# A feature-crossing tower: layer 0's sums as full matmuls, its last tile beside a half tile of layer 1, and another front

## The chip, the cores and the metric

The kernel runs on one core of one Trainium2 chip. The metric is the device time of one execution in microseconds, lower is better. Its engines are TensorE (PE in the profile, its weight loads PEld), VectorE (DVE), ScalarE (ACT), GpSimd (POOL) and SyncE (SP), which here only issues DMAs. SP, ACT and POOL each issue DMAs in their own order; each engine works through its instructions in program order.

## The reference, cut to what matters

512 rows, 39 fields, each looked up in a table of its own: `e` is 512 x 39 x 16.

```python
z0 = einsum('bid,bjd->bdij', x0, x0)           # 39*39 products
cur0 = relu(einsum('bdk,kl->bld', z0, W0))      # l = 128
next_h, direct0 = split(cur0, 2, axis=1)        # 64 and 64
z1 = einsum('bid,bjd->bdij', x0, next_h)        # 39*64 products
cur1 = relu(einsum('bdk,kl->bld', z1, W1))
z = sum(concatenate([direct0, cur1], axis=1), axis=-1)
h = concatenate([z, dense_ctx], axis=1)         # 192 + 16
h = relu(h @ W_top1 + b_top1); h = relu(h @ W_top2 + b_top2); y = h @ W_top3
```

## The kernel before, in words

The batch is cut into 16 chunks (`CHUNKS`) of 32 rows; with 16 components each, a chunk has N = 512 columns. In every chunk:

- **Bringing x.** GpSimd gathers 11 times per chunk into `found` (L282; 117 partitions = 3 sets of 39 fields). ScalarE's `split` (L289) rounds it to `found_hi`, VectorE's `split` (L393) makes `found_lo`, the rest. SP lays high part, low part and the full values out in a DRAM buffer `x_rows` (`lay_out` L190, six DMAs; `full_rows` L213, three), and reads from it twice: `place` (L199) brings both parts to `x_parts` in four DMAs, and `widen` (L224) copies four fields at a time to 64 partitions each in `x_wide`, six DMAs of 512 KB per chunk. Buffers are three deep. `bring` (L244) is one chunk's `lay_out`, `full_rows` and `place`.
- **Layer 0.** It rests on squares: a product of two fields is had from the square of their sum. `add_up` (L476) makes sums of pairs of fields on PE with a 0/1 matrix, two tiles ("a duo") at a time: each of the two matmuls has 64 rows only, since the fields are placed so that one half of the partitions serves each tile; the seventh tile takes all 128 rows. ScalarE's `square` (L296) squares them to SBUF and `contract0` (L489) contracts them with `w0`, both operands float32. `evict0` (L303) makes `h` (twice, on both halves) and `direct`.
- **Layer 1.** 20 tiles in five groups of four. VectorE's `multiply` (L415) makes z = x * h for a group. x comes from `x_wide` (groups 0, 2, 4) or from PSUM, where PE's `spread_out` (L499, four matmuls of 32 rows) puts it (groups 1, 3). For groups 0 to 3 ScalarE makes `z_hi` (`high_part` L320) and VectorE `z_lo` (`low_part`), and PE contracts z_hi with w1_hi and w1_lo (`contract1_hi` L510, eight matmuls) and z_lo with w1_hi (`contract1_lo` L521, four). Group 4 is taken whole in float32 (`contract1_whole` L529). z, z_hi and z_lo are rings of three. 39 x 64 rows are 19.5 tiles, so the 20th is half zeros. `evict1` and two reductions on VectorE end the chunk.
- **Order.** It is written out by hand for every engine. PE works in group g of chunk c on layer 1 of c and on layer 0 of c+1: one duo's `contract0` and the next duo's `add_up` in each of groups 0 to 3. A low part is contracted one group after its high part. ScalarE has `split(1)` ahead of `evict0(0)` in the front, and `split(c+3)` at the end of group 4 of chunk c.
- **End.** `hid1_of`, `hid2_of` and `y_of` (L537 to L569) are the three top layers, for 480 columns early (their first layer inside chunk 15) and for the last 32 late.

## Time and profile before

| | |
|---|---|
| median of 3 runs | 449.84 us (449.59 to 449.95) |
| the profiled execution | 449.96 us, of which the span is 448.1 |
| PE busy | 91% of the span |
| VectorE, ScalarE, GpSimd busy | 78%, 51%, 60% |
| moved by DMA | 64.03 MB, mean 143 GB/s |

The span is what the profiler records from the first instruction to the last. An engine's busy time says how much of it the engine worked, not whether the end waited for it; that is told by the chain of work that ended last. The timeline gives the start and the length of instructions; the length of a matmul includes its way through the array, so what it takes in a row of its like is read from the distance of the starts. The granted clock of PE is 1.00 for 2.4 GHz and 0.50 for 1.2 GHz.

### The profile page before, as it was taken

The page shows a single profiled execution, that of the slowest core. Times are in us where ns is not written, and L with a number is a line of the kernel's source. Part 1 is how long each engine was busy: PE and PEld are TensorE (multiplying, and loading weights), DVE is VectorE, ACT ScalarE, POOL GpSimd, SP SyncE. Part 2 cuts the span into 40 slices and gives each one's busy share as a digit, 9 for nine tenths or more (in the row PEclk, how much of TensorE's full clock was granted, in tenths as well). Part 3 has the DMA queues.
Part 4 walks back from the last instruction along what each step waited for, and adds up shares of the span by engine and source line. Part 5 has one row for each costly group of instructions (what it writes and reads, how often), then busy time and mean ns, then how long its engine had stood idle before and what let it go on. Part 6 is the DMA issues. An engine that isn't in the chain of part 4 may idle for free.

```text
span 448.1 us, 4257 instructions
## 1 busy us (share of the span) xinstructions
PE 405.8 (91%) x1446; PEld 238.8 (53%) x1446; DVE 347.6 (78%) x197; ACT 227.2 (51%) x224; POOL 270.8 (60%) x180
## 2 busy tenths in 40 slices
PE   0263299999999999999999999999999999999997
PEld 0221056565656565656565565656565656565744
DVE  0301676998989898989898989899898989998900
ACT  2122346556464646465564655655646464645413
POOL 5777888888888888888888888888810000000000
PEclk9958589999999999999999999999999999999999
DMA  8369269493959495868668596959493949752000
GB/s 286 97 152 182 43 145 186 108 213 84 216 117 216 100 205 107 198 136 196 133 155 171 138 193 143 188 125 208 98 211 84 218 96 212 165 129 59 1 0 0
DMA packets 25740, 64.03 MB, mean 143 GB/s; under 512 B 8512, under 2 KB 16661, under 8 KB 19446
## 3 DMA queue, kind: packets, MB, share of 16 engines
q1 hardware_dynamic: 19128, 60.55, 60.4%
q0 software_dynamic: 5632, 1.35, 3.2%
q10 hardware_dynamic: 958, 1.86, 1.2%
q8 instruction: 11, 0.18, 0.2%
q14 instruction: 11, 0.09, 0.1%
HBM read 59.87 MB, written 3.84 MB: 142 GB/s over the span
## 4 chain that ended last, share of the span: by engine, by line
PE 87%; issue 8%; SPq 4%; DMA 0%; ACT 0%
PE acc L495 22%; PE acc L525 14%; PE acc L517 13%; PE acc L518 13%; PE acc L533 12%; PE sums L485 5%; PE spread L506 3%; PE spread L562 2%; SPq L243 1%; SPq L232 1%; SPq L195 1%; SPq L221 0%; PE sums L551 0%; PE sums L553 0%; SPq L205 0%
## 5 line engine op out<-in xcount | busy, mean ns | idle before, releaser
L282 POOL DMA_INDIRECT found<-in_table_dram,rows_sb x176 | 270.6, 1538 | 56.6 <-issue 53.0
L423 DVE TENSOR_TENSOR z_lo<-z,z_hi 128x2048 fp32r<-128x2048 f32 x64 | 146.2, 2285 | 2.3 <-ACT z_hi L325 1.3
L325 ACT ACTIVATE z_hi<-z 128x2048 fp32r<-128x2048 f32 x64 | 122.3, 1911 | 16.8 <-DVE z L415 15.0
L415 DVE TENSOR_TENSOR z<-x_wide,h 128x2048 f32<-128x2048 f32 x48 | 109.8, 2288 | 12.5 <-ACT h L309 8.7
L495 PE MATMUL acc<-squares,w 128*128 128x512 f32 x224 | 114.7, 631 | 0.0
L517 PE MATMUL acc<-z_hi,w_hi 128*128 128x512 f32 x256 | 106.9, 417 | 0.7 <-ACT cur L318 0.7
L518 PE MATMUL acc<-z_hi,w_lo 128*128 128x512 f32 x256 | 100.3, 392 | 0.0
L301 ACT ACTIVATE squares<-sums 128x1024 f32<-128x1024 f32 x64 | 58.8, 919 | 78.7 <-PE sums L485 70.7
L525 PE MATMUL acc<-z_lo,w_hi 128*128 128x512 f32 x256 | 90.5, 475 | 0.0
L415 DVE TENSOR_TENSOR z<-spread,h 128x2048 f32<-128x2048 f32 x32 | 73.1, 2283 | 1.3 <-PE spread L506 1.2
L525 PEld LDWEIGHTS acc<-z_lo,w_hi 128*128 128x128 f32 x256 | 47.0, 188 | 32.3 <-issue 26.8
L495 PEld LDWEIGHTS acc<-squares,w 128*128 128x128 f32 x224 | 39.7, 194 | 37.9 <-issue 36.5
L533 PE MATMUL acc<-z,w_sb 128*128 128x512 f32 x128 | 57.5, 592 | 0.0
L517 PEld LDWEIGHTS acc<-z_hi,w_hi 128*128 128x128 f32 x256 | 48.4, 189 | 15.5 <-issue 3.9
L518 PEld LDWEIGHTS acc<-z_hi,w_lo 128*128 128x128 f32 x256 | 48.3, 189 | 13.9 <-issue 3.9
L485 PE MATMUL sums<-x_parts,select_sb 64*128 64x512 f32 (+1 forms) x112 | 31.9, 507 | 23.7 <-DMA x_parts<-x_rows 22.2
L398 DVE TENSOR_TENSOR found_lo<-found,found_hi 117x176 fp32r<-117x176 f32 x16 | 5.5, 343 | 45.4 <-issue 23.6
L485 PEld LDWEIGHTS sums<-x_parts,select_sb 64*128 64x128 f32 (+1 forms) x112 | 12.4, 191 | 47.5 <-issue 46.9
L533 PEld LDWEIGHTS acc<-z,w_sb 128*128 128x128 f32 x128 | 24.3, 190 | 24.3 <-issue 23.0
L308 ACT ACTIVATE h<-acc 64x512 f32<-64x512 f32 x16 | 9.5, 593 | 52.5 <-PE acc L495 52.5
L318 ACT ACTIVATE cur<-acc 128x512 f32<-128x512 f32 x16 | 9.6, 598 | 34.2 <-issue 20.0
L434 DVE TENSOR_REDUCE feat_a<-cur 128x32 f32<-128x512 f32 x16 | 10.9, 681 | 8.7 <-ACT cur L318 8.7
(41 smaller groups left out, 111.2 us busy)
## 6 DMA issues: line engine op xcount, KB each, us to landing
x_wide<-x_rows SPq DMA_DIRECT2D x96, 512.0 KB
x_parts<-x_rows SPq DMA_DIRECT2D x62, 64.0 KB
found<-in_table_dram,rows_sb POOLq DMA_INDIRECT x176
w_sb<-in_w_dram SPq DMA_DIRECT2D x1, 1280.0 KB, 7.2
x_rows<-found_hi SPq DMA_DIRECT2D x32, 26.8 KB
x_rows<-found SPq DMA_DIRECT2D x32, 26.8 KB
x_rows<-found_lo SPq DMA_DIRECT2D x30, 26.8 KB
z<-in_select_dram ACTq DMA_DIRECT2D x1, 576.0 KB, 7.9
```

Source lines behind the costliest of these rows:

```text
L282: pool.indirect_dma_start(out=found[:, b, s * D:s * D + D], out_offset=None, in_=table, in_offset=bass.IndirectOffsetOnAxis(ap=rows_sb[:, ...
L301: nc.scalar.activation(squares[:, q % RING0, 0:n, :], sums[:, 0:n, :], ACT.Square).then_inc(squared, 1)
L325: nc.scalar.activation(z_hi[:, n % RING], z[:, n % RING], ACT.Copy).then_inc(hi_done, 1)
L415: nc.vector.tensor_tensor(z[:, n % RING], x, h[:, c % 2, :].unsqueeze(1).to_broadcast([P, QUADS, N]), ALU.mult).then_inc(multiplied, 1)
L423: nc.vector.tensor_tensor(z_lo[:, n % RING], z[:, n % RING], z_hi[:, n % RING], ALU.subtract).then_inc(lo_done, 1)
L485: last = nc.tensor.matmul(sums[:, a, :], select_sb[rows, t, :], x_parts[rows, c % BUFS, :], start=True, stop=True)
L495: last = nc.tensor.matmul(acc0[:, :], w0[:, t, :], squares[:, q % RING0, a, :], start=(t == 0), stop=(t == T0 - 1))
L506: last = nc.tensor.matmul(spread[:, q, :], select_sb[rows, T0 + i, :], x_parts[rows, c % BUFS, :], start=True, stop=True)
L517: nc.tensor.matmul(acc1[:, :], w1_hi[:, t, :], z_hi[:, r, a, :], start=(t == 0), stop=False)
L518: last = nc.tensor.matmul(acc1[:, :], w1_lo[:, t, :], z_hi[:, r, a, :], start=False, stop=False)
L525: last = nc.tensor.matmul(acc1[:, :], w1_hi[:, QUADS * g + a, :], z_lo[:, r, a, :], start=False, stop=False)
L533: last = nc.tensor.matmul(acc1[:, :], w1_sb[:, VT + a, :], z[:, r, a, :], start=False, stop=(a == QUADS - 1))
```

## The change: what it does

- x_parts is placed otherwise (`STEP`, `rows_of`): the fields of every quarter of the partitions overlap, and each field has its two parts in at least one. `add_up` takes all 128 rows for every tile, so that the matmuls of a duo follow each other on the full array.
- The squares' tiles are filled densely (`pairs`): six full ones, and a seventh with 12 pairs, which stand in rows 64 to 127. `contract0` of the seventh tile has 64 rows, as has its `square`. It is called within `contract1_whole`, right behind the half tile of layer 1, which now takes rows 0 to 63 alone; the whole group is group 2 now, not 4.
- The groups whose x comes from PSUM are 0 and 3. The order of layer 0's steps moves by one duo: in groups 0 and 1 the duos 1 and 2 of chunk c+1 are contracted, in group 2 the last tile, in group 4 duo 0 of chunk c+2. The low part of group 4 is contracted in the next chunk, and in the last chunk between the two halves of `hid2_of`.
- `found` has three planes (high, low, full). `lay_out` writes all three with one DMA for each set (3 instead of 9), `place` takes two DMAs instead of four; both wait for the low part. `x_rows` has a 40th row, which a DMA fills once.
- The front: `keep_busy` puts 30 matmuls ahead of chunk 0's first sum and 14 behind its `contract0`; `evict0(0)` stands ahead of `split(1)`; `split(1)` on VectorE stands behind `multiply(0)`; the high part of group 0 is contracted before chunk 1's sums; the third `widen` of chunk 0 comes after `bring(1)`.

```diff
--- before.py
+++ after.py
...
+STEP = 8
...
-QSTART = [0, 16, 7, 23]
...
-SPREAD = [1, 3]
-WIDE = [0, 2, 4]
-SPREAD_FROM = [0, 24, 12, 36]
...
+SPREAD = [0, 3]
+WIDE = [1, 2, 4]
+SPREAD_FROM = [0, 4, 32, 12]
+WIDE_FROM = [[8, 16], [28, 35], [20, 24]]
...
+WHOLE = 2
...
+def rows_of(f):
+    return [2 * QUADS * (f - STEP * q) + 2 * q for q in range(QUADS) if 0 <= f - STEP * q < 2 * STEP]
...
+    order = [(f, f) for f in range(F)] + [(i, j) for i in range(F) for j in range(i + 1, F)]
+    return [order[P * t:P * t + P] for t in range(T0)]
...
-        def lay_out(queue, c, half):
-            b = c % BUFS
-            queue.wait_ge((found_hi_done, found_lo_done)[half], c + 1)
-            for s, w in enumerate(SET_COLS):
-                queue.dma_start(x_rows[b, half, :, GW * s:GW * s + w],
-                                (found_hi, found_lo)[half][F * s:F * s + F, b, 0:w].bitcast(F32)
-                                ).then_inc(rows_out[b], 16)
...
-        def place(queue, c, quads):
-            b = c % BUFS
-            queue.wait_ge(rows_out[b], 16 * 6 * uses(c))
-            for q in quads:
-                start = x_rows[b, 0, QSTART[q], 0:1]
-                queue.dma_start(x_parts[32 * q:32 * q + 32, b, :].bitcast(F32),
-                                bass.AP(start.tensor, start.offset, [[N, QF], [F * N, 2], [1, N]])
-                                ).then_inc(placed[b], 16)
...
+            def lay_out(c):
...
-                sp.wait_ge(gathered[b], 16 * SLOTS * uses(c))
-                if c >= BUFS:
-                    for i in range(len(WIDE)):
-                        sp.wait_ge(wide_in[i], 32 * (c - BUFS + 1))
+                sp.wait_ge(found_lo_done, c + 1)
                 for s, w in enumerate(SET_COLS):
-                    sp.dma_start(x_rows[b, 2, :, GW * s:GW * s + w],
-                                 found[F * s:F * s + F, b, 0:w]).then_inc(full_out[b], 16)
+                    start = x_rows[b, 0, 0, GW * s:GW * s + 1]
+                    sp.dma_start(bass.AP(start.tensor, start.offset, [[N, F], [FR * N, 3], [1, w]]),
+                                 found[F * s:F * s + F, b, :, 0:w]).then_inc(rows_out[b], 16)
+            def place(c):
+                b = c % BUFS
+                sp.wait_ge(rows_out[b], 16 * SETS * uses(c))
+                for half in range(2):
+                    start = x_rows[b, half, 0, 0:1]
+                    sp.dma_start(x_parts[half:P:2, b, :].bitcast(F32),
+                                 bass.AP(start.tensor, start.offset, [[N, 2 * STEP], [STEP * N, QUADS], [1, N]])
+                                 ).then_inc(placed[b], 16)
...
+            def bring(c):
+                if c >= BUFS:
+                    sp.wait_ge(placed[c % BUFS], 32 * uses(c - BUFS))
+                    sp.wait_ge(multiplied, G * (c - BUFS + 1))
+                lay_out(c)
+                if c >= BUFS:
+                    sp.wait_ge(spread_done, len(SPREAD) * (c - BUFS + 1))
+                    sp.wait_ge(summed, ND * (c - BUFS + 1))
+                place(c)
...
-            for i in range(len(WIDE)):
-                widen(0, i)
+            sp.wait_ge(filler_in, 16)
+            bring(0)
+            widen(0, 0)
+            widen(0, 1)
             bring(1)
+            widen(0, 2)
             bring(2)
...
-                    pool.wait_ge(full_out[b], 16 * SETS * uses(c - BUFS))
+                    pool.wait_ge(rows_out[b], 16 * SETS * uses(c - BUFS))
                 for s in range(SLOTS):
...
             def split(c):
                 b = c % BUFS
                 act.wait_ge(gathered[b], 16 * SLOTS * uses(c))
-                if c >= BUFS:
-                    act.wait_ge(rows_out[b], 16 * 6 * uses(c - BUFS))
-                nc.scalar.activation(found_hi[:, b, :], found[:, b, :], ACT.Copy).then_inc(found_hi_done, 1)
+                nc.scalar.activation(found[:, b, 0, :].bitcast(F32R), found[:, b, 2, :],
+                                     ACT.Copy).then_inc(found_hi_done, 1)
...
                 n = len(DUOS[q % ND])
+                rows = slice(0, P) if n == 2 else slice(HALF, P)
                 act.wait_ge(summed, q + 1)
                 if q >= RING0:
                     act.wait_ge(contracted0, q - RING0 + 1)
-                nc.scalar.activation(squares[:, q % RING0, 0:n, :], sums[:, 0:n, :], ACT.Square).then_inc(squared, 1)
+                nc.scalar.activation(squares[rows, q % RING0, 0:n, :], sums[rows, 0:n, :], ACT.Square).then_inc(squared, 1)
             def evict0(c):
...
             act.dma_start(base_sb[:, :], base).then_inc(ids_in, 16)
             act.dma_start(select_in, select).then_inc(select_in_done, 16)
+            filler = x_rows[0, 0, F, 0:1]
...
             split(0)
-            lay_out(act, 0, 1)
-            place(act, 0, [2, 3])
             for d in range(ND):
                 square(d)
+            evict0(0)
             split(1)
-            evict0(0)
             high_part(0)
+            high_part(1)
             square(ND)
+            square(ND + 1)
             for c in range(CHUNKS):
                 for g in range(G):
                     n = G * c + g
                     if g == 0 and c:
                         evict1(c - 1)
-                    if n == 0:
+                    if g < 2 and c + 1 < CHUNKS:
+                        square(ND * (c + 1) + 2 + g)
+                    if g > 2 and c + 2 < CHUNKS:
+                        square(ND * (c + 2) + g - 3)
+                    if 0 < n < G * CHUNKS - 1 and is_v(n + 1):
+                        high_part(n + 1)
+                    if g == 2 and c + 1 < CHUNKS:
+                        evict0(c + 1)
+                    if n == 1:
                         split(2)
-                    if c + 1 < CHUNKS and g < ND - 1:
-                        square(ND * (c + 1) + g + 1)
-                    if c + 1 < CHUNKS and g == ND - 1:
-                        evict0(c + 1)
-                        if c + 2 < CHUNKS:
-                            square(ND * (c + 2))
-                    if n + 1 < G * CHUNKS and is_v(n + 1):
-                        high_part(n + 1)
                     if g == G - 1 and c + BUFS < CHUNKS:
                         split(c + BUFS)
-                    if c == CHUNKS - 1 and g >= 2:
-                        for m in [[0], [1], [2, 3]][g - 2]:
+                    if c == CHUNKS - 1 and g > 2:
+                        for m in [[0, 1], [2, 3]][g - 3]:
                             hid1_act(m, early)
...
+            hid2_act(0, early)
             evict1(CHUNKS - 1)
-            for m in range(M2 // P):
-                hid2_act(m, early)
+            hid2_act(1, early)
...
             dve.wait_ge(mixed, 1)
-            nc.vector.tensor_copy(w0[0:32, 0, :], acc1[0:32, 0:P]).then_inc(w0_ready, 1)
-            nc.vector.tensor_copy(w0[0:F - 32, 1, :], acc1[32:F, 0:P]).then_inc(w0_ready, 1)
...
                                     ALU.subtract).then_inc(w1_lo_ready, 1)
-            split(1)
             dve.wait_ge(select_ready, 1)
             multiply(0)
-            reduce0(0)
+            split(1)
             for c in range(CHUNKS):
                 for g in range(G):
                     n = G * c + g
@@ -462,6 +446,8 @@
                     if is_v(n):
                         low_part(n)
                     if n == 0:
+                        reduce0(0)
+                    if n == 1:
                         split(2)
...
-                for a, t in enumerate(tiles):
-                    rows = slice(HALF * a, HALF * a + HALF) if len(tiles) == 2 else slice(0, P)
-                    last = nc.tensor.matmul(sums[:, a, :], select_sb[rows, t, :], x_parts[rows, c % BUFS, :],
+                for a, t in enumerate(DUOS[q % ND]):
+                    last = nc.tensor.matmul(sums[:, a, :], select_sb[:, t, :], x_parts[:, c % BUFS, :],
                                             start=True, stop=True)
                 last.then_inc(summed, 1)
+            def keep_busy(acc, count):
+                for _ in range(count):
+                    nc.tensor.matmul(acc[:, :], select_sb[:, 0, :],
+                                     select_sb[:, 0:N // P, :].rearrange("p t m -> p (t m)"), start=True, stop=True)
...
                 pe.wait_ge(squared, q + 1)
+                rows = slice(0, P) if d < ND - 1 else slice(HALF, P)
                 for a, t in enumerate(DUOS[d]):
-                    last = nc.tensor.matmul(acc0[:, :], w0[:, t, :], squares[:, q % RING0, a, :],
+                    last = nc.tensor.matmul(acc0[:, :], w0[rows, t, :], squares[rows, q % RING0, a, :],
                                             start=(t == 0), stop=(t == T0 - 1))
...
-            def contract1_whole(n):
+            def contract1_whole(n, beside):
                 r = n % RING
                 pe.wait_ge(multiplied, n + 1)
-                for a in range(QUADS):
+                nc.tensor.matmul(acc1[:, :], w1_sb[0:HALF, VT, :], z[0:HALF, r, 0, :], start=False, stop=False)
+                if beside is not None:
+                    contract0(beside)
+                for a in range(1, QUADS):
                     last = nc.tensor.matmul(acc1[:, :], w1_sb[:, VT + a, :], z[:, r, a, :],
-                                            start=False, stop=(a == QUADS - 1))
+                                            start=False, stop=False)
                 last.then_inc(contracted1, 1)
...
             last.then_inc(mixed, 1)
             pe.wait_ge(select_ready, 1)
+            keep_busy(acc0, 30)
             add_up(0)
-            pe.wait_ge(w0_ready, 3)
-            spread_out(SPREAD[0])
+            spread_out(0)
+            pe.wait_ge(w0_ready, 2)
...
+            keep_busy(acc1, 14)
...
                     n = G * c + g
-                    if (n + 2) % G in SPREAD and SPREAD[0] < n + 2 < G * CHUNKS:
+                    if n == 0:
+                        contract1_hi(0)
+                        add_up(ND)
+                        add_up(ND + 1)
+                        contract0(ND)
+                    elif g == 0:
+                        contract1_lo(n - 1)
+                    if (n + 2) % G in SPREAD and n + 2 < G * CHUNKS:
                         spread_out(n + 2)
-                    if n == 0:
-                        add_up(ND)
-                    if c + 1 < CHUNKS and g < ND:
-                        if ND * (c + 1) + g + 1 < ND * CHUNKS:
-                            add_up(ND * (c + 1) + g + 1)
-                        contract0(ND * (c + 1) + g)
+                    if g < 2 and c + 1 < CHUNKS:
+                        add_up(ND * (c + 1) + 2 + g)
+                        contract0(ND * (c + 1) + 1 + g)
+                    if g > 2 and c + 2 < CHUNKS:
+                        add_up(ND * (c + 2) + g - 3)
+                    if g == G - 1 and c + 2 < CHUNKS:
+                        contract0(ND * (c + 2))
                     if c == CHUNKS - 1 and g >= 2:
                         for m in [[0], [1], [2, 3]][g - 2]:
                             hid1_of(m, early)
-                    if n and is_v(n - 1):
+                    if g and is_v(n - 1):
                         contract1_lo(n - 1)
-                    if is_v(n):
+                    if n and is_v(n):
                         contract1_hi(n)
-                    else:
-                        contract1_whole(n)
-            for m in range(M2 // P):
-                hid2_of(m, early)
...
```

## Rows read from the trace of the kernel before

**Rows 1.** The page: span, TensorE's busy share, its granted clock in 40 slices.

```profile
span 448.1 us, 4257 instructions
...
PE 405.8 (91%) x1446; PEld 238.8 (53%) x1446; DVE 347.6 (78%) x197; ACT 227.2 (51%) x224; POOL 270.8 (60%) x180
...
PEclk9958589999999999999999999999999999999999
```

**Rows 2.** The page: the chain that ended last, shares by engine.

```profile
PE 87%; issue 8%; SPq 4%; DMA 0%; ACT 0%
```

**Rows 3.** Windows, one chunk: length, PE, PEld, DVE, ACT, POOL, clock, DMA, GB/s.

```profile
84.62:108.27 23.65, 23.65 (x86) 14.00 (x85) 21.46 (x13) 13.52 (x13) 19.99 (x13) 1.00 0.74 156
```

**Rows 4.** Timeline, TensorE within one chunk: start us, us, engine, line, operation.

```profile
249.85 0.39 PE L518 MATMUL acc<-z_hi,w_lo 128*128 128x512 f32 x1
...
250.17 0.50 PE L506 MATMUL spread<-x_parts,select_sb 32*128 32x512 f32 x4
...
250.60 0.51 PE L485 MATMUL sums<-x_parts,select_sb 64*128 64x512 f32 x2
...
251.04 1.98 PE L495 MATMUL acc<-squares,w 128*128 128x512 f32 x4
...
252.46 1.49 PE L525 MATMUL acc<-z_lo,w_hi 128*128 128x512 f32 x4
...
253.79 0.39 PE L517 MATMUL acc<-z_hi,w_hi 128*128 128x512 f32 x1
...
255.63 0.39 PE L485 MATMUL sums<-x_parts,select_sb 128*128 128x512 f32 x1
...
255.86 1.88 PE L495 MATMUL acc<-squares,w 128*128 128x512 f32 x4
```

**Rows 5.** Chain that ended last, in order of time: the group taken whole.

```profile
266.26 3.43 PE acc L533 x8
```

**Rows 6.** Timeline, VectorE: two steps in a row.

```profile
83.27 2.28 DVE L415 TENSOR_TENSOR z<-x_wide,h 128x2048 f32<-128x2048 f32 x1
85.47 2.29 DVE L423 TENSOR_TENSOR z_lo<-z,z_hi 128x2048 fp32r<-128x2048 f32 x1
```

**Rows 7.** Timeline of the front, all engines and the queues that issue DMAs.

```profile
15.44 3.21 PE L576 MATMUL acc<-w,mix_sb 128*39 128x128 f32 x14 [15.44 <-DMA mix_sb<-in_mix_dram]
...
20.09 1.20 ACTq L195 DMA_DIRECT2D x_rows<-found_lo  x3
...
26.04 0.80 PE L485 MATMUL sums<-x_parts,select_sb 64*128 64x512 f32 x2 [7.40 <-DMA x_parts<-x_rows]
...
34.85 2.74 PE L495 MATMUL acc<-squares,w 128*128 128x512 f32 x6
...
41.73 0.35 ACT L294 ACTIVATE found_hi<-found 117x176 fp32r<-117x176 f32 x1 [6.09 <-DMA found<-in_table_dram,rows_sb]
...
43.27 2.29 DVE L415 TENSOR_TENSOR z<-x_wide,h 128x2048 f32<-128x2048 f32 x1 [0.82 <-ACT h L308]
...
52.43 0.80 PE L485 MATMUL sums<-x_parts,select_sb 64*128 64x512 f32 x2 [14.85 <-DMA x_parts<-x_rows]
...
60.99 0.50 PE L506 MATMUL spread<-x_parts,select_sb 32*128 32x512 f32 x4
```

**Rows 8.** Windows of the front, columns as in rows 3.

```profile
37.00:42.00 5.00, 0.58 (x2) 0.00 (x0) 0.00 (x0) 0.27 (x2) 3.78 (x5) 1.00 1.01 196
...
29.00:42.00 13.00, 8.58 (x17) 3.04 (x16) 0.00 (x0) 2.71 (x5) 9.95 (x11) 0.87 1.03 208
52.40:59.00 6.60, 5.45 (x9) 2.45 (x10) 3.51 (x3) 4.09 (x4) 5.38 (x5) 0.50 0.20 41
```

**Rows 9.** Timelines: last gathers of chunks 1 and 3, and chunk 3's split.

```profile
32.56 1.00 POOL L282 DMA_INDIRECT found<-in_table_dram,rows_sb  x1 [0.30 <-issue]
...
68.30 1.90 POOL L282 DMA_INDIRECT found<-in_table_dram,rows_sb  x1 [0.30 <-issue]
...
78.25 0.33 ACT L294 ACTIVATE found_hi<-found 117x176 fp32r<-117x176 f32 x1
```

100 lines of the change are left out of this document (39 added, 61 removed).

## Prediction

> **What bounds the kernel now.** I read the page first: TensorE (PE) is busy for 91% of the span, and its granted clock is full from the seventh slice of 11.2 us on [rows 1]. The chain of work that ended last is 87% PE [rows 2]: the reader is to see that nothing else sets the length of the middle. The busy times of one chunk (of 16) say the same: PE 23.65 of 23.65 us, VectorE 21.46, ScalarE 13.52, GpSimd 19.99, the DMA engines 0.74 [rows 3]. So there are two places for time to go: a chunk of 23.65 us, which repeats, and the front, where PE stands still.
>
> **What a chunk of PE consists of.** From its timeline [rows 4]:
> - A matmul of z_hi, z_lo or a full sum costs 0.228 us when its like follows: the single full sum starts at 255.63, the next at 255.86. There are 48 of the former (4 groups of 8 + 4).
> - Both operands float32: two records each. Eight of them take 3.43 us in the chain [rows 5], 0.429 each. There are 22: 14 of layer 0's seven tiles, 8 of the group that is taken whole.
> - Matmuls on 64 or 32 rows come as groups (2 or 4 start together). spread at 250.17, sums at 250.60, contract0 at 251.04: 0.44 a group. What is lost around such an island: the last full matmul starts at 249.85 and streams until 250.08. Four z_lo matmuls start behind contract0 and end at 253.79, so they began at 252.88 and contract0's four records at 251.16. From 250.08 to 251.16 are 1.08 us for two groups, so 0.20 on top of 0.88.
>
> Per chunk: 48 x 0.228 + 22 x 0.429 + one full sum 0.23 + four islands x 0.20 + five groups x 0.44 (three sums, two spreads) = 10.94 + 9.44 + 0.23 + 0.80 + 2.20 = 23.6, which is the 23.65 measured.
>
> **Part 1, sums over all rows.** Three pairs at 0.44 become six full matmuls at 0.228 (1.32 to 1.37: the pairs themselves bring nothing), but only the two spreads stay islands: two islands less, 0.40, and 0.05 given back. Gain 0.35 per chunk, in the 15 chunks that do layer 0 for another. Sure, since both forms are in the rows.
>
> **Part 2, the last tile beside the half tile.** Layer 0's seventh tile has 12 pairs now and takes rows 64 to 127; layer 1's half tile takes rows 0 to 63. Both were full float32 matmuls: 4 x 0.429 = 1.72 per chunk. No row shows float32 on 64 rows, so the cost is bounded. The issue order is A1 A2 B1 B2 (two records each, each with its weight load). If A and B lie wholly beside each other: 2 x 0.429 + 0.20 = 1.06. If the order is kept, A2 and B1 overlap and no more: 3 x 0.429 + 0.20 = 1.49. If nothing overlaps: 1.92. If also a weight load is exposed inside the island (an estimate of 0.2, what an island loses around it): 2.1. I take 1.49, because the pairs of sums do overlap [rows 4] and nothing shows a later matmul passing an earlier one. Gain 0.23 per chunk, between +0.66 and -0.4.
>
> The Trainium skill, "TensorE: Matmul & The Clock Gate", section "Measured speedup vs the span model", has packed tiles take one matmul's time plus about 4 ns a tile. By it the pair costs 1.06 and the forecast would be 6.5 us lower; this is a rival below. The same page says that matmuls start and end in program order, which speaks for 1.49. "TensorEngine Tiling (Array Packing)", section "Key Properties", says that a change of tiling mode drains the engine; the 0.20 of an island agrees with it, and it speaks against part 2, which makes an island of its own.
>
> New chunk: 48 x 0.228 + 18 x 0.429 + 1.49 + 7 x 0.228 + two islands and spreads 1.28 = 23.03. Against 23.65 that is 0.6, times 15 = **9.2 us** (between -6 and +15.5).
>
> **Does something else become the bound?** VectorE's steps follow each other at 2.20 us [rows 6]; nine, two reductions and one split are 21.4 per chunk, 1.6 below the new PE. I followed the new order from PE's group 3 (T): multiply of group 0 ends at T+3.1, its low part at T+11.4 (PE asks at T+14.7), group 1's low part at T+15.8 to 16.5 (asked T+17.4). The waits with least room: add_up at group 4 needs the square of the sum at group 3. ScalarE has the high part of group 3 and three evictions (1.8) before it, done about when PE reaches group 3; then the square is ready 1.7 us after the sum, and PE comes after 2.3. evict1 waits for the low part moved to the next chunk, and behind PE's wait lie a sum and a contract0, 2.2 us, against eviction and latency, 0.7. So the order costs nothing while these margins (0.6 to 0.9) last. evict0 comes a group earlier, so the wait for h falls; it cost PE nothing. DMA moves the same bytes.
>
> **Part 3, the front.** Now: x of chunk 0 is summed at 26.04, contract0 is through at 34.85 + 6 x 0.429 = 37.4, but ScalarE has split(1) ahead of evict0(0), and the gathers of chunk 1 land only at 41.73; multiply(0) starts at 43.27, and PE waits until 52.43 for x of chunk 1, 14.85 us of it idle [rows 7]. The clock is 0.50 from 52.4 to 59 [rows 8], so the first sums, contract0(4) and group 0's high part end at 60.9 [rows 7].
> New: the mixing matmuls end at 18.65 [rows 7]; with one more DMA ahead of w0 say 19.1. keep_busy's 30 matmuls take 6.8 at full clock, 13.7 at half; I take the rise in the middle, 28.0 (x itself is there at about 26: laid out by three DMAs behind the low part, 20.1 + 1.2 + the 4.75 us that now lie between the last lay-out issue, 21.29, and the sum). Then at full clock: sum and spread, square 1.0, contract0 in four steps, to 37.0; evict0(0) follows at once, to 38.9; multiply(0) 38.3 to 40.5; split(1) behind both, 40.8. This needs the gathers of chunk 1: the last is issued at 32.56 [rows 9], and of x_wide 2 MB instead of 3 are under way, at 208 GB/s [rows 8] done by about 37. Five DMAs in place of ten for chunk 1: 40.9 + 1.2 + 4.75 = 46.9. Group 0's high part (about 42.5 to 44.3) is done by then, and the 14 keep_busy matmuls (3.2) end at about 40, before it. Sum, square, sum, contract0(4): 50.8 at full clock. Against 60.9: **10.1 us**. Bounds: keep_busy ends at 26.1 or 32.8 (+2, -5, one for one, since split(1) stands behind evict0(0)); the clock falls in the two gaps of some 2 us around hi(0), -3 (against it: with the last matmul at 37.4 it was 1.00 until 42 [rows 8]); gathers of chunk 1 behind x_wide as now, -2.8.
>
> **What is late next.** GpSimd is not faster: the last gather of chunk 3 is issued at 68.30 [rows 9]. Now split(3) comes at 78.25, without a wait [rows 9]. New, PE is at group 3 of chunk 0 at 50.8 + 12.5 = 63.3, and ScalarE reaches split(3) at 68.5. The gather lands at 71.7 (1.5 us after its end, as for chunk 0), or at 75, if it queues behind the 3 MB of x_wide that SP issues from 58.6 on, behind bring(2). ScalarE stands in that wait with evict1(0) behind it, VectorE in its own split(3) with multiply(6) behind it. Four steps of 2.20 later group 6's low part is ready at 80.9 or 83.6; PE wants it at 80.7. With a smaller repeat at chunk 4: 0.2 to 5, I take **3 us** lost. GpSimd needs 20.0 per chunk [rows 3] and leads afterwards.
>
> **End.** Chunk 14 has no sums for a later chunk, so PE falls to 20.4 there, under VectorE's pace: 0.7; a half tile alone in the last chunk 0.2. The last low part slides between the two halves of hid2 with PE's work unchanged. **1 us** lost.
>
> **Sum.** 9.2 + 10.1 - 3 - 1 = 15.3. The profiled execution took 449.96 (span 448.1 and 1.86 around it); the median of the runs is 449.84, 0.1 less. 449.96 - 15.3 = 434.6, so 434.5.
>
> **Rivals.**
> 1. The pair doesn't overlap (1.92 to 2.1): for it, an island shows 0.20 lost around it, and no float32 pair is seen; against, the pairs of sums overlap. Costs 6.5 to 9: 441 to 443.5.
> 2. The pair overlaps wholly (1.06): 15 x 0.43 = 6.5 less: 428.
> 3. The front gives back half: the clock is low, or chunk 1 or 3 comes late for the reasons above: 5 to 7 lost, 440 to 441.
> 4. Slower: ScalarE's split(c+3) stands ahead of evict1 and VectorE's ahead of multiply. If a chunk's gathers take more than PE's chunk, this wait recurs in every chunk. GpSimd is 20.0 of 23.65 busy; its instructions take 1.00 us, or 1.90 when transfers are under way [rows 9]. It decides from 23.65 per chunk on; at 25, 13 chunks x 2 = 26 lost against 15 gained plus the front's: about 452. Against it: now it never waits and still gains on PE.
>
> **How the numbers follow.** Forecast (431 to 438) 0.45; rival 1, 0.22; rival 2, 0.12; rival 3, 0.17; rival 4, 0.04. Range 427 to 444 holds all but rival 4 and combinations of 1 and 3. Beyond 0.2% (0.9 us, about what can be told from no change): faster 0.94, within 0.02, slower 0.04.
>
> **What would show it.** A chunk of 23.0 us in the windows; sums as full matmuls at 0.23 steps; the start of the float32 pair to the next whole matmul 1.3 to 1.5; PE's first sum of chunk 1 at 47 with clock 1.0; ScalarE waiting for gathers at split(3) only. Wrong would be: a chunk of 23.5 (no overlap), a clock of 0.5 after 45, waits of PE for squares, or of ScalarE for gathers in every chunk.

## The result and the profile after

The changed kernel takes 441.73 us (median of 4 runs, 441.18 to 444.44), the kernel before 449.89 beside it (449.59 to 450.14): 8.2 us less by the medians. The ratio that counts every run is 0.9832, 95% interval 0.9807 to 0.9857, which is 7.6 us. 15.4 were forecast: the time is inside the range, the gain about half. The profiled execution took 441.91, its span is 439.9; against the 448.1 of the kernel before that is again 8.2, and the parts below are read from these two executions.

The page of the changed kernel, the lines that answer to [rows 1] and [rows 2]:

```profile
span 439.9 us, 4140 instructions
...
PEclk9989799999999999999999999999999999999899
...
PE 76%; POOL 12%; issue 5%; DVE 3%; DMA 3%; ACT 0%; DVEq 0%
```

The chain was 87% PE; now GpSimd holds 12% of it and VectorE and the DMA 3% each. PE is no longer alone in setting the length. The clock falls in slice 5 (44 to 55 us) and a little in slices 3 (22 to 33) and 38 (407 to 418).

Windows of the changed kernel, columns as in [rows 3]: one chunk, two stretches of the front (beside [rows 8]), the last chunk:

```profile
160.00:182.88 22.88, 22.88 (x86) 14.19 (x86) 21.53 (x13) 13.37 (x14) 19.53 (x12) 1.00 0.77 164
...
37.00:48.40 11.40, 6.99 (x26) 4.27 (x24) 8.56 (x6) 5.85 (x6) 9.28 (x7) 1.00 0.27 60
48.40:55.40 7.00, 5.85 (x10) 3.06 (x11) 3.37 (x2) 2.05 (x2) 6.24 (x3) 0.58 0.67 138
...
404.00:406.00 2.00, 0.63 (x3) 0.19 (x1) 2.00 (x2) 0.00 (x0) 0.00 (x0) 1.00 0.00 0
...
408.00:410.00 2.00, 2.00 (x5) 1.07 (x4) 2.00 (x2) 1.21 (x1) 0.00 (x0) 0.50 0.00 0
```

A chunk is 22.88 us with PE busy throughout. To see where the 8.2 went, one event is followed through both kernels: PE's start on the high part of group 3, in chunks 0, 1, 13 and 15. Timeline of the kernel before:

```profile
73.54 0.39 PE L517 MATMUL acc<-z_hi,w_hi 128*128 128x512 f32 x1
...
97.20 0.39 PE L517 MATMUL acc<-z_hi,w_hi 128*128 128x512 f32 x1
...
380.96 0.39 PE L517 MATMUL acc<-z_hi,w_hi 128*128 128x512 f32 x1
...
424.01 0.39 PE L517 MATMUL acc<-z_hi,w_hi 128*128 128x512 f32 x1
```

and of the changed one:

```profile
68.85 0.39 PE L511 MATMUL acc<-z_hi,w_hi 128*128 128x512 f32 x1
...
94.99 0.39 PE L511 MATMUL acc<-z_hi,w_hi 128*128 128x512 f32 x1
...
369.59 0.40 PE L511 MATMUL acc<-z_hi,w_hi 128*128 128x512 f32 x1
...
416.08 0.77 PE L511 MATMUL acc<-z_hi,w_hi 128*128 128x512 f32 x1
```

| part | forecast | measured | from |
|---|---|---|---|
| front, to chunk 0 | +10.1 | +4.7 | 73.54 - 68.85 |
| chunk 0 to 1 | -3 | -3.3 | 26.14 against 22.88 |
| 15 chunks | +9.2 | +11.5 | 15 x (23.65 - 22.88) |
| end | -1 | -4.7 | last two periods: 43.05 before, 46.49 after (of 47.30 and 45.76 by the steady pace), -5.0; tail 24.1 and 23.8, +0.3 |
| sum | 15.3 | 8.2 | |

Of the four terms the first and the last are far off, and the third is 2.3 too small. The first two belong together, as the runs show: 1.4 in place of 7.1.

### The profile page after: what moved, and what is told of

It reads as the page before. It is cut to its first block, busy times and chain, and to the rows that moved or that the text cites. A ratio compares the mean times of both kernels' runs of the same rounds, so it can differ in the third digit from the quotient of the medians.

```text
span 439.9 us, 4140 instructions
## 1 busy us (share of the span) xinstructions
PE 407.8 (93%) x1490; PEld 250.4 (57%) x1490; DVE 347.9 (79%) x196; ACT 225.7 (51%) x224; POOL 285.5 (65%) x180
## 3 DMA queue, kind: packets, MB, share of 16 engines
q0 software_dynamic: 5632, 1.35, 3.1%
## 4 chain that ended last, share of the span: by engine, by line
PE 76%; POOL 12%; issue 5%; DVE 3%; DMA 3%; ACT 0%; DVEq 0%
PE acc L487 15%; POOL found L266 12%; PE acc L519 12%; PE acc L512 11%; PE acc L511 11%; PE acc L530 9%; PE sums L470 6%; PE acc L526 4%; PE spread L500 3%; DVE z_lo L409 3%; DMA found<-in_table_dram,rows_sb 2%; PE spread L559 2%; PE sums L550 1%; DVE z L401 1%; DMA base_sb<-in_base_dram 1%
## 5 line engine op out<-in xcount | busy, mean ns | idle before, releaser
L266 POOL DMA_INDIRECT found<-in_table_dram,rows_sb x176 | 285.3, 1621 | 56.7 <-issue 53.3
L487 PE MATMUL acc<-squares,w 128*128 128x512 f32 (+1 forms) x224 | 111.2, 614 | 0.0
L519 PE MATMUL acc<-z_lo,w_hi 128*128 128x512 f32 x256 | 83.3, 447 | 1.8 <-DVE z_lo L409 1.8
L519 PEld LDWEIGHTS acc<-z_lo,w_hi 128*128 128x128 f32 x256 | 48.5, 191 | 26.2 <-issue 15.1
L487 PEld LDWEIGHTS acc<-squares,w 128*128 128x128 f32 (+1 forms) x224 | 42.4, 195 | 29.2 <-issue 25.4
L470 PE MATMUL sums<-x_parts,select_sb 128*128 128x512 f32 x112 | 42.8, 453 | 5.8 <-DMA x_parts<-x_rows 3.9
L530 PE MATMUL acc<-z,w_sb 128*128 128x512 f32 x96 | 45.5, 610 | 0.0
L530 PEld LDWEIGHTS acc<-z,w_sb 128*128 128x128 f32 x96 | 16.9, 189 | 27.4 <-issue 27.4
L470 PEld LDWEIGHTS sums<-x_parts,select_sb 128*128 128x128 f32 x112 | 20.3, 195 | 18.6 <-issue 9.9
L420 DVE TENSOR_REDUCE feat_a<-cur 128x32 f32<-128x512 f32 x16 | 10.9, 680 | 13.9 <-ACT cur L302 13.9
L526 PE MATMUL acc<-z,w_sb 64*128 64x512 f32 x32 | 18.1, 647 | 0.0
L384 DVE TENSOR_TENSOR found<-found 117x176 fp32r<-117x176 f32 x16 | 5.5, 342 | 15.4 <-issue 9.5
```

Source lines behind the costliest of these rows:

```text
L266: pool.indirect_dma_start(out=found[:, b, 2, s * D:s * D + D], out_offset=None, in_=table, in_offset=bass.IndirectOffsetOnAxis(ap=rows_sb[ ...
L470: last = nc.tensor.matmul(sums[:, a, :], select_sb[:, t, :], x_parts[:, c % BUFS, :], start=True, stop=True)
L487: last = nc.tensor.matmul(acc0[:, :], w0[rows, t, :], squares[rows, q % RING0, a, :], start=(t == 0), stop=(t == T0 - 1))
L519: last = nc.tensor.matmul(acc1[:, :], w1_hi[:, slot1(g) + a, :], z_lo[:, r, a, :], start=False, stop=(g == G - 1 and a == QUADS - 1))
L526: nc.tensor.matmul(acc1[:, :], w1_sb[0:HALF, VT, :], z[0:HALF, r, 0, :], start=False, stop=False)
L530: last = nc.tensor.matmul(acc1[:, :], w1_sb[:, VT + a, :], z[:, r, a, :], start=False, stop=False)
```

## The experiments

The edits are to the changed kernel, unless said. "Whole group" is PE's first matmul of three full tiles in `contract1_whole` (L530); in the changed kernel it stands at 65.07 in chunk 0, 91.22 in chunk 1, then every 22.88, and 388.69 and 412.16 at the end. "The last period" is the distance of these two, 23.47. Behind each time stand its lowest and highest run, then the ratio to the kernel before, measured beside it, and the ratio's 95% interval. Theories at the start: the clock, low in the front and at the end, took the gain (the clock theory); or chunk 3's gathers and a wait in the last chunk did (the queue theory). The letters in the recorded expectations are each run's own.

One thing has to be known before the traces are compared: the same code doesn't get the same clock in every execution. e11 leaves the front as it is, and its chunk 0 has its whole group at 61.49, 3.6 earlier. e1 and e8 leave the end as it is, and their last period is 21.88. So the place of chunk 0, and 1.6 us in the last period, can differ without an edit.

### The steady chunk: the pair alone, and the sums alone

e6 gives the pair full matmuls again:

```diff
-                rows = slice(0, P) if n == 2 else slice(HALF, P)
+                rows = slice(0, P)
...
-                rows = slice(0, P) if d < ND - 1 else slice(HALF, P)
+                rows = slice(0, P)
...
-                nc.tensor.matmul(acc1[:, :], w1_sb[0:HALF, VT, :], z[0:HALF, r, 0, :], start=False, stop=False)
+                nc.tensor.matmul(acc1[:, :], w1_sb[:, VT, :], z[:, r, 0, :], start=False, stop=False)
```

> The changed kernel with part 2 undone: half tile and last tile take all 128 rows each (zeros in the other half), in the same places of the order. Theory A (the pair really overlaps: 1.26 us for it and what is lost around it, where two full float32 matmuls take 1.72): a chunk takes 23.34 us and the time rises by 6 to 7 us, to about 448. Rival (the pair gains nothing and the chunk's 22.88 come from the sums): 22.9, no change.

Measured: 447.45 us (445.69 to 448.15; ratio 0.9957, 0.9940 to 0.9974), a chunk of 23.38. The pair is worth 0.50 per chunk, 7.5 in all; the time rose by 5.7, since in its profile the last period was 21.5 and not 23.47, with a clock of 1.00. Timelines of PE, e6:

```profile
252.57 1.02 PE L526 MATMUL acc<-z,w_sb 128*128 128x512 f32 x2
...
254.28 1.02 PE L530 MATMUL acc<-z,w_sb 128*128 128x512 f32 x2
```

and the changed kernel:

```profile
249.36 1.07 PE L519 MATMUL acc<-z_lo,w_hi 128*128 128x512 f32 x4
250.35 0.69 PE L526 MATMUL acc<-z,w_sb 64*128 64x512 f32 x1
250.36 0.69 PE L487 MATMUL acc<-squares,w 64*128 64x512 f32 x1
250.89 0.59 PE L526 MATMUL acc<-z,w_sb 64*128 64x512 f32 x1
250.90 0.59 PE L487 MATMUL acc<-squares,w 64*128 64x512 f32 x1
251.41 2.84 PE L530 MATMUL acc<-z,w_sb 128*128 128x512 f32 x6
```

In e6 the four records are a row of full ones, 252.57 to 254.28. In the changed kernel the first record of both stands at 250.35, the second of both at 250.89: A1 and B1 side by side, then A2 and B2, though they are issued A1 A2 B1 B2.

e7 is the kernel before, with all sums on 128 rows (part 1 alone; the halves of the partitions then both count, so its sums are others):

```diff
-                    rows = slice(HALF * a, HALF * a + HALF) if len(tiles) == 2 else slice(0, P)
+                    rows = slice(0, P)
```

> The kernel before with one edit: add_up's matmuls take all 128 rows (the selection matrix has zeros in the other half). It is part 1 alone. Theory A (only the two islands around the sums are saved): a chunk takes 23.3 us instead of 23.65 and the time is 444.5 to 445. Rival (VectorE or a wait takes the place): 23.65 and 449.8.

Measured: 445.63 (444.72 to 445.98; 0.9905, 0.9885 to 0.9924), a chunk of 23.35: 0.30 per chunk. The time fell by 3.8 against the 449.44 beside it, a little less than the 15 x 0.30 = 4.5. With the 0.50 of the pair that is 0.80, for 0.77 measured.

### The end

e2 calls hid1_of(0) one group later, so that PE doesn't wait for a reduction ahead of a low part; e3 keeps the wait and fills it with matmuls; e11 moves the reduction.

```diff
-                        for m in [[0], [1], [2, 3]][g - 2]:
+                        for m in [[], [0, 1], [2, 3]][g - 2]:
                             hid1_of(m, early)
```

> The changed kernel, with the first tile of the top layer for the early columns (hid1_of(0), which waits for chunk 14's reduction on VectorE) moved from group 2 to group 3 of the last chunk. Theory A (PE's wait of 2.2 us at 404.5 in the last chunk, and the half clock that follows it, cost some 4.5 us of the end): the clock stays at 1.00 through the last chunk and the time falls by 3.5 to 5 us, to 437 to 438. Theory B (the last chunk is at VectorE's pace anyway, so a wait only moves): under 1 us.

Measured: 439.87 (438.55 to 441.5; 0.9771, 0.9748 to 0.9795). In the profiled execution, the longest of its four, the last period is 19.67 with 1.38 us of waiting for the low part, and the clock still fell to 0.56 from 408 to 410. That period isn't comparable with 23.47, since the tile's work now stands behind the whole group: the profiled execution took 441.50, only 0.4 less than the changed kernel's. By the medians it is 1.9 less, where 3.5 to 5 or under 1 had been expected, so e2 decides neither.

```diff
                     pe.wait_ge(mlp_in, 16 * 8)
+                    pe.wait_ge(squared, ND * CHUNKS)
+                    keep_busy(hid1_acc[0], 9)
```

> The changed kernel, with nine filler matmuls (2.1 us) into the same PSUM bank ahead of the wait of hid1_of(0) in the last chunk. The wait itself stays. If the clock that falls behind that wait is worth 2 to 3 us by itself, the time falls by that, to about 439; if only the wait counts, the time stays at 441.7.

Measured: 440.73 (439.95 to 443.85; 0.9819, 0.9777 to 0.9860). From 408 to 410, where the changed kernel has 0.50, its window reads

```profile
408.00:410.00 2.00, 2.00 (x8) 1.12 (x7) 2.00 (x2) 1.01 (x1) 0.00 (x0) 1.00 0.00 0
```

and the last period is 21.88 in place of 23.47. That the filler matmuls did this isn't shown. e1 and e8 (below) leave the last chunk as it is, PE waits the same 2.19 us ahead of hid1_of(0), and their last period is 21.88 too; the same window of e1:

```profile
408.00:410.00 2.00, 2.00 (x8) 0.92 (x6) 2.00 (x2) 1.44 (x1) 0.00 (x0) 1.00 0.00 0
```

In e4, e5 and e10, which leave it as it is too, the clock fell and the last period is 23.46 to 23.55. So the price of the fall is 1.6 us, and whether the clock falls behind this wait differs between executions. The wait itself is still there in e3, under the filler matmuls.

```diff
-                    if g == 1 and c:
+                    if g == 1 and 0 < c < CHUNKS - 1:
                         reduce1(c - 1)
+                    if n == G * (CHUNKS - 1):
+                        reduce1(c - 1)
```

> The changed kernel with one edit: in the last chunk VectorE's reduction of chunk 14 stands behind the low part of group 0 instead of group 1, so that hid1_of(0) finds it done and PE works on it in the gap at 404.5. Theory A (PE's wait and the half clock behind it are the end's loss): no wait of PE over 1.5 us in the last chunk, clock 1.00, the time falls by 3 to 4.5 us against the changed kernel, to 437.5 to 438.7. Rival (VectorE's pace sets the last chunk): within 1 us of 441.7, or only the 1.4 us that the fillers of e3 gave.

Measured: 439.31 (437.67 to 440.68; 0.9783, 0.9757 to 0.9809); the last period 20.10, clock 1.00 there, waits of PE for low parts 0.9. So at the end 3.4 us lay in one wait (21.88 - 20.10 = 1.8) and in the clock behind it (23.47 - 21.88 = 1.6). The last period is 20.1 in the profiles of all five kernels with this edit (e9, e11 to e14). By the medians e11 gains 2.4, less than the 3 to 4.5 expected; its four runs lie wide apart, two near 438 and two above 440, and the profiled one is the fastest.

### The front: is it the clock?

e1 keeps the clock up with more filler matmuls (22 in place of 14, and 8 behind the first high part); e8 takes all fillers out.

```diff
-            keep_busy(acc1, 14)
+            keep_busy(acc1, 22)
...
                         contract1_hi(0)
+                        pe.wait_ge(evicted0, 1)
+                        keep_busy(acc0, 8)
                         add_up(ND)
```

> The changed kernel, with TensorE kept at work in the front: 22 filler matmuls ahead of group 0's high part instead of 14, and 8 more between it and chunk 1's first sum. Theory A (the gathers of chunk 3 bind the start: they land at 79.45 and ScalarE and VectorE stand in split(3) until then): the clock stays at 1.00 from 48 to 56 and contract0 of chunk 1 ends about 2.5 us earlier, but the first whole group of chunk 1 still starts at 91.2 and the time stays at 441.7 (within 0.7). Theory B (the half clock from 48 to 55 is what the front lost): the time falls by 2.5 to 3 us, to about 439.

Measured: 440.21 (439.35 to 441.4; 0.9792, 0.9769 to 0.9815). From 48.4 to 55.4 the clock is 1.00, not 0.58, and chunk 0's whole group stands at 61.90, 3.2 earlier. Chunk 1's stands at 91.05, 0.2 earlier: 3.0 of 3.2 are gone one chunk later. The time is 1.5 us under the changed kernel's, between the two expectations; in the profiled executions 1.6 of the difference is the last period (21.88), which this edit doesn't touch. Its ScalarE timeline:

```profile
79.28 0.35 ACT L276 ACTIVATE found<-found 117x176 fp32r<-117x176 f32 x1 [7.87 <-DMA found<-in_table_dram,rows_sb]
```

> The changed kernel without any filler matmuls in the front. Theory A (gathers bind): the first sums and contract0 run at half clock, chunk 0's whole group starts 1 to 3 us later than 65.07, its distance to chunk 1's shrinks by about as much, and the time stays within 1 us of 441.7. Rival (the fillers bring what they look like): 3 us slower, 444.7.

(e8 leaves out `keep_busy(acc0, 30)` and `keep_busy(acc1, 14)`.) Measured: 440.01 (439.35 to 444.47; 0.9817, 0.9761 to 0.9873), whole groups at 64.91 and 91.08. Chunk 0 was expected 1 to 3 us later and wasn't; that the time is 1.7 us lower is again the last period, 21.88. The fillers of the change bring nothing that can be measured. With a clock of 0.58, 1.00 and 0.56 from 48.4 to 55.4 chunk 1 stands at 91.22, 91.05 and 91.08, so the clock theory falls for the front: something else holds chunk 1 at 91.1.

### The front: chunk 3's gathers

That is ScalarE's `split(3)`. The changed kernel, timelines of SP's queue, GpSimd and ScalarE (the gather at 70.47 is the 44th, chunk 3's last; 68.30 in [rows 9] is the same one):

```profile
64.07 3.79 SPq L219 DMA_DIRECT2D x_wide<-x_rows  x6
...
70.47 1.00 POOL L266 DMA_INDIRECT found<-in_table_dram,rows_sb  x1 [0.30 <-issue]
...
79.45 0.35 ACT L276 ACTIVATE found<-found 117x176 fp32r<-117x176 f32 x1 [4.85 <-DMA found<-in_table_dram,rows_sb]
```

Its chain of waits has this step between the gather's issue and split(3):

```profile
70.47 8.67 DMA found<-in_table_dram,rows_sb
```

e10 leaves out 7 of the 11 gathers in each of chunks 3 to 5 (on top of e1's fillers):

```diff
+        def slots(c):
+            return 4 if 3 <= c <= 5 else SLOTS
...
-                for s in range(SLOTS):
+                for s in range(slots(c)):
```

> Leaves work out: chunks 3, 4 and 5 gather only 4 of their 11 blocks of rows (the rest of their values is that of older chunks). Otherwise the changed kernel with e1's filler matmuls. Theory A (e1's 3.2 us are lost only because the gathers of chunk 3 land late): the whole groups of chunks 0 and 1 lie 22.9 apart instead of 29.15, the whole group of chunk 1 starts near 84.8 and the time falls by 6 us against e1, to about 434.2. Rival (something else in chunk 0 or 1 holds PE: x of chunk 2 or 3 on its way through DRAM, x_wide): the distance stays over 26 and the time over 437.

Measured: 434.04 (433.21 to 435.06; 0.9661, 0.9642 to 0.9680). `split(3)` starts at 69.47 without a wait, the whole groups stand at 60.05, 82.94 and 105.80. That is 6.2 us under e1. The edit thins chunks 4 and 5 too, but chunk 1's whole group at 82.94, 8.1 earlier than in e1, stands ahead of anything that waits for these: chunk 3's gathers are what the front's gain is lost to.

e4 moves split(3), on ScalarE and VectorE, into group 1 of chunk 1 (n == G + 1); e12 puts it into group 0 (n == G), with e11's edit. On each of the two engines e4's edit reads:

```diff
+                    if n == G + 1:
+                        split(3)
-                    if g == G - 1 and c + BUFS < CHUNKS:
+                    if g == G - 1 and 0 < c and c + BUFS < CHUNKS:
                         split(c + BUFS)
```

> The changed kernel, with split(3) on ScalarE and VectorE moved from group 4 of chunk 0 to group 1 of chunk 1, so that nothing stands behind the gathers of chunk 3. Theory A (the 26.15 us from chunk 0's to chunk 1's whole group against 22.88 later are the wait for these gathers): that distance falls to 22.9 to 23.5 and the time by 2.5 to 3.3, to about 438.8. Rival (x of chunk 3 then comes too late for the sums at group 3 of chunk 1, or PE is what is late there): the loss comes back one chunk later and the time stays within 1 us.

Measured: 446.36 (444.42 to 446.49; 0.9927, 0.9910 to 0.9943), 4.6 slower, where 3 faster or no change had been expected. The whole groups stand at 61.72, 84.58 and 116.63: chunk 1 has its 22.86, and the loss comes back in the next one at 9.2. Timelines of GpSimd and VectorE in e4:

```profile
72.02 9.09 POOL L266 DMA_INDIRECT found<-in_table_dram,rows_sb  x1 [0.30 <-issue]
81.41 0.99 POOL L266 DMA_INDIRECT found<-in_table_dram,rows_sb  x1 [0.30 <-issue]
...
75.75 2.27 DVE L403 TENSOR_TENSOR z<-x_wide,h 128x2048 f32<-128x2048 f32 x1
...
81.00 2.27 DVE L403 TENSOR_TENSOR z<-spread,h 128x2048 f32<-128x2048 f32 x1
```

Without its wait VectorE works from 71.35 to 80.16 on operations that read both inputs from SBUF, and one gather lies on GpSimd for 9.09 us beside them. The next takes 0.99 beside an operation whose x comes from PSUM (81.00).

> e11's edit, and split(3) on ScalarE and VectorE in group 0 of chunk 1 (in e4 it stood in group 1), behind multiply(6) and the low part of group 5. Theory A (GpSimd is held up by VectorE's run of operations with two SBUF inputs): the gathers of chunk 3 come later by the two operations that now stand ahead, some 2 to 4 us; chunks 0 and 1 lie 23 to 25 apart, but part of the gain is given back at chunk 1 to 2: between 1.5 us faster and 2 us slower than e11. Rival (e4's 9 us were an accident of its place): 3.3 us faster than e11, about 435.

Measured: 437.79 (437.59 to 438.45; 0.9744, 0.9727 to 0.9760), whole groups at 61.51, 85.63, 113.32: again what chunk 1 gains (24.12) chunk 2 gives back (27.69). It is 1.5 under e11 by the medians and equal to it in the profiled executions (437.59 and 437.67).

e5 tests the gathers' length alone: three operations of VectorE with both inputs in SBUF are put into the front, where it has nothing to do and chunk 1's gathers run.

```diff
+            for k in range(RING):
+                nc.vector.tensor_tensor(z_lo[:, k, :, :].rearrange("p a n -> p (a n)"),
+                                        w1_sb[:, 0:VT, :].rearrange("p t m -> p (t m)"),
+                                        w1_hi[:, :, :].rearrange("p t m -> p (t m)"), ALU.subtract)
```

> The changed kernel, with three more VectorE operations in the front (float32 subtractions with both inputs in SBUF, 2.2 us each), right behind the one at 20.8, where VectorE stands idle and GpSimd's gathers take 1.00 us. Nothing waits for them. Theory A (a gather's instruction on GpSimd is held up while VectorE runs an operation with two SBUF inputs): between 23 and 30 the gathers take 1.9 us or more each, or one of them 4 to 9 us, and all later ones come 3 to 6 us later. Theory B (gathers are slow when transfers of x_wide are under way): the gathers between 23 and 30 stay at 1.00 us.

Measured: 443.57. It is one run, so the trace is what counts here and not the time. Its timelines of VectorE and GpSimd:

```profile
23.04 6.70 DVE L438 TENSOR_TENSOR z_lo<-w_sb,w_hi 128x2048 fp32r<-128x2048 f32 x3
...
24.31 1.90 POOL L266 DMA_INDIRECT found<-in_table_dram,rows_sb  x1 [0.30 <-issue]
26.51 1.89 POOL L266 DMA_INDIRECT found<-in_table_dram,rows_sb  x1 [0.30 <-issue]
...
30.91 1.00 POOL L266 DMA_INDIRECT found<-in_table_dram,rows_sb  x1 [0.30 <-issue]
```

Three gathers take 1.9 in place of 1.0, the next 1.00 again, with the same transfers still running. GpSimd falls 2.7 behind, split(3) comes at 81.34 and chunk 1's whole group 1.9 later: less than the 3 to 6 expected, the mechanism as expected.

e9 has e1's and e11's edits together.

> e11's edit with e1's filler matmuls in the front. If the gathers of chunk 3 bind the front, e1's part adds only the 0.2 us that the whole group of chunk 1 gained: within 0.7 us of e11. If the clock counts, 2.5 us or more below it.

Measured: 437.75 (437.08 to 438.21; 0.9737, 0.9721 to 0.9754), split(3) at 78.79 with 7.43 of waiting, chunk 3's last gather issued at 72.14. It is 1.6 under e11 by the medians, where at most 0.7 or at least 2.5 had been expected, so these decide neither; the two profiled executions are equal (437.63 and 437.67), with chunk 1's whole group at 90.57 and 90.38.

That left open why a gather issued at 70.47 lands at 79.1. The DMA queues of the changed kernel (packets, MB, share of the 16 engines), from 64 to 74 and from 74 to 84; q0 carries the gathers, 32 packets each (5632 for 176), q1 the rest:

```profile
q1 hardware_dynamic: 436, 2.13, 95.9%
q0 software_dynamic: 60, 0.02, 1.5%
...
q1 hardware_dynamic: 594, 1.52, 69.6%
q0 software_dynamic: 310, 0.07, 7.0%
```

While the 3 MB of x_wide run, not two gathers get through in 10 us; as they end, ten do. Two causes are left for a late landing: the gather is issued late (theory I), or its transfer crawls beside the x_wide traffic (theory D). e13 issues the first third of chunk 1's x_wide ahead of bring(2), e14 fills x_wide of chunk 1 for one field of four and so leaves work out (both on e9).

```diff
+            widen(1, 0)
             bring(2)
             for c in range(CHUNKS - 1):
-                for i in range(len(WIDE)):
+                for i in range(0 if c else 1, len(WIDE)):
                     widen(c + 1, i)
```

> The kernel of e9, with the first third of chunk 1's x_wide (1 MB) issued right behind the last third of chunk 0's, ahead of bring(2), instead of at 61.3 with the two others. Open is what makes the last gather of chunk 3 late at ScalarE's split(3) (78.79 in e9, 7.43 us of waiting): that GpSimd issues it late (theory I), or that, once issued (about 70, with a record of 1 to 2 us), its transfer crawls behind the 3 MB of x_wide that SP issues at 61.3 and lands when they end (theory D). D: 2 MB are left behind 61 instead of 3, so they end 5 us earlier; split(3) at 73.5 to 75, whole group of chunk 1 at 85.5 to 87 instead of 90.6; time 433.5 if nothing is given back at chunk 2, 437 if chunk 4's gathers take it back as in e12. I: the issue of the gathers doesn't move, split(3) stays at 78.8 and the time at 437.7. Either way the gathers of chunk 2 may land up to 3 us later, since another 1 MB runs before 56.

Measured: 436.50 (435.27 to 437.39; 0.9726, 0.9700 to 0.9753). split(3) and the whole group of chunk 1 (87.39) come 0.6 and 0.4 later than theory D had them at the latest, and 3.2 earlier than theory I. Its ScalarE timeline:

```profile
75.62 0.35 ACT L277 ACTIVATE found<-found 117x176 fp32r<-117x176 f32 x1 [3.48 <-DMA found<-in_table_dram,rows_sb]
```

> The kernel of e9, but chunk 1's x_wide is filled for one field of four only (0.75 MB instead of 3; the other columns keep what chunk 0 left there, so the results of chunk 1 are not the reference's); everything else is as in e9. Theory D (the gather's transfer lands behind the x_wide traffic): with that traffic gone, the last gather of chunk 3 lands 1.5 to 2.5 us after its issue ends, split(3) at 71.5 to 73.5 with a wait under 2 us, whole group of chunk 1 at 84.7 to 86; time 432 to 433 if nothing is given back at chunk 2, 436 to 437 if it is. Theory I (late issue alone): split(3) stays at 78 to 79, time 437.7. GpSimd's records may still show 2 to 9 us for single gathers while VectorE works with both inputs in SBUF; that they do, with split(3) early, would say that these records are not what bound chunk 3, but may bind chunk 4.

Measured: 435.04 (434.91 to 435.37; 0.9689, 0.9664 to 0.9714). Its GpSimd and ScalarE timelines:

```profile
72.17 1.00 POOL L267 DMA_INDIRECT found<-in_table_dram,rows_sb  x1 [0.30 <-issue]
...
74.47 0.35 ACT L277 ACTIVATE found<-found 117x176 fp32r<-117x176 f32 x1 [3.08 <-DMA found<-in_table_dram,rows_sb]
```

In e14 the same gather is issued when it was in e9 (72.17 and 72.14) and is in ScalarE's hands 4.3 earlier, 1.3 behind its end. Theory D holds, by somewhat less than expected (split(3) 1 us later than its latest, the time between its two forecasts): 4.3 us of the wait are the traffic. What is left of the wait is theory I, the issue at 72.17 with the gathers before it held up (68.80 takes 3.06). The whole groups stand at 61.87 and 86.24 in e14, 59.68 and 87.39 in e13, so 4.3 and 3.2 earlier than e9's 90.57, and 2.6 and 2.4 of that are left in the last chunk.

e13 is the fastest version that computes everything: 5.2 us under the change, 13.1 under the kernel before. Its interval overlaps e9's and e12's, so that it beats these is likely, not shown.

## Why the prediction was right or wrong

**Sums over all rows: right.** 0.35 per chunk forecast, 0.30 in e7. Two islands less, no more.

**The pair: the right kind, mis-sized.** I took 3 x 0.429 + 0.20 = 1.49 because nothing showed a later matmul passing an earlier one. It takes 1.14 by the rows (the four z_lo matmuls begin at 249.36 and stream for 4 x 0.228, until 250.27; the full ones start at 251.41) and 1.22 by the chunk (1.72 less the 0.50 of e6). The step that failed is "if the order is kept, A2 and B1 overlap and no more". Rival 2 had the mechanism, at 1.06 with the island, some 0.1 too low. The chunk is 0.15 shorter than forecast, and the term 9.2 became 11.5. The lower bound of that term, -6, was added up wrongly: it leaves out part 1's gain, and with the pair at 2.1 and part 1 at 0.35 the fifteen chunks come to about nothing. The Trainium skill, "TensorE: Matmul & The Clock Gate", section "Measured speedup vs the span model", has packed tiles at one matmul's time plus some 4 ns each. The trace agrees in that A and B start 0.01 apart in both passes; the distance of the passes (0.54) is more than a full record's 0.43, which the page doesn't cover.

**Other engines in the steady chunk: right.** No wait of PE in 160 to 182.88; the margins of 0.6 to 0.9 held.

**The front, 10.1: wrong by 3.1 at its own place** (contract0(4) is through at 53.9, not 50.8) **and by 5.5 at group 3's high part** (68.85, not 63.3). Three steps of it, and one that cost nothing:
- "Then at full clock" failed twice, the first time in chunk 0. x came at 27.52, ahead of the 28.0 that I had allowed, and contract0 was through only at 38.4, not 37.0. PE had waited 1.74 for x. In e11, whose front is the same, it waited 0.22, and from x to the end of contract0 it took 9.5 in place of 10.9. Windows of the changed kernel and of e11:

```profile
27.00:34.00 7.00, 5.71 (x15) 3.09 (x16) 0.00 (x0) 2.23 (x3) 5.48 (x6) 0.76 1.04 224
...
27.00:34.00 7.00, 6.23 (x21) 3.14 (x20) 0.00 (x0) 3.59 (x4) 5.30 (x6) 1.00 1.02 216
```

  So multiply(0) started at 39.84, not 38.3, VectorE's split(1) stood behind it as planned, at 42.05, and x of chunk 1, forecast for 46.9, came at 48.44: 1.5.
- The second time is chunk 1: the clock is 0.58 from 48.4 on, behind a wait of 2.32 ahead of the high part and of 2.13 ahead of the sums. The bound of -3 named this, and I argued it away with the 1.00 until 42 in [rows 8], a row of another stretch. From the first sum to chunk 0's whole group are 16.6 us, in e1, at a clock of 1.00, 13.7: 2.9.
- The 12.5 from contract0(4) to group 3's high part was carried over from the order of before. In the new order it takes 13.7 in e1, without a wait and at full clock (51.94 to 65.67): 1.2.
- keep_busy ended at 25.8, not 28.0, since the clock was up already (1.00 from 12 to 18.6). e8: the fillers cover nothing.

**What is late next, -3: the mechanism right, the step that failed is its start.** I had the last gather behind "the 3 MB of x_wide that SP issues from 58.6 on", landing at 75. It did queue there, and took nearly the time that I gave it: 16.4 forecast from x_wide's issue to the gather's landing, 15.1 measured. But x_wide was issued at 64.07, 5.5 later than I had it, since it stands behind bring(2), and that behind the splits of chunk 2 at 59.37. So the landing came at 79.1. As T had slipped too (the high part of group 3 at 68.85), the wait came out at 4.85 and the loss at 3.3, close to the 3: two errors that cancel, and so luck. e1 takes one away: with chunk 0 3.2 earlier the loss is 29.15 - 22.88 = 6.3. So front and stall are one term: chunk 1 starts when chunk 3's gathers land, and what PE gains before that counts nothing. Treating 10.1 and -3 as separate terms was the real fault; their sum was 1.4, not 7.1.

I also carried GpSimd's times over from before, 68.30 for the last gather. It was issued at 70.47: 0.8 of these 2.2 us were there at chunk 1's last gather already (33.38 against 32.56), 1.4 came later. Gathers were held up in the kernel before too: from chunk 1's last to chunk 3's it took 35.7 us, the changed kernel 37.1, and 22 gathers of 1.00 with 0.30 between them would take 28.7. New is how early it happens: most of it lies between 42 and 53, timelines of VectorE and GpSimd in the changed kernel:

```profile
42.30 2.29 DVE L401 TENSOR_TENSOR z<-x_wide,h 128x2048 f32<-128x2048 f32 x1
44.50 2.28 DVE L409 TENSOR_TENSOR z_lo<-z,z_hi 128x2048 fp32r<-128x2048 f32 x1
46.70 0.67 DVE L414 TENSOR_REDUCE feat_b<-direct 64x32 f32<-64x512 f32 x1
47.30 2.27 DVE L401 TENSOR_TENSOR z<-x_wide,h 128x2048 f32<-128x2048 f32 x1
49.49 2.28 DVE L409 TENSOR_TENSOR z_lo<-z,z_hi 128x2048 fp32r<-128x2048 f32 x1
...
42.50 2.96 POOL L266 DMA_INDIRECT found<-in_table_dram,rows_sb  x1 [0.30 <-issue]
45.76 1.90 POOL L266 DMA_INDIRECT found<-in_table_dram,rows_sb  x1 [0.30 <-issue]
47.96 4.69 POOL L266 DMA_INDIRECT found<-in_table_dram,rows_sb  x1 [0.30 <-issue]
52.95 0.99 POOL L266 DMA_INDIRECT found<-in_table_dram,rows_sb  x1 [0.30 <-issue]
```

Three gathers take 9.55 in place of 3 while VectorE, brought forward, works from SBUF; the fourth, with VectorE idle, 0.99. "1.90 when transfers are under way" was a wrong reading of [rows 9]: e5 shows that it is VectorE. Without these 6.5 us the last gather would be issued at 63.9, just ahead of x_wide at 64.07; that is an estimate by subtraction, and no run shows it. How much of the 3.3 is theirs and how much is the traffic's can't be split: e5 (2.7 later on GpSimd, 1.9 later in chunk 1) and e14 (4.3 earlier without the traffic) each move it alone.

The Trainium skill, "SBUF — State Buffer", section "Who interferes with whom", says that a VectorE instruction with two SBUF inputs contends with a GpSimd instruction that reads SBUF. A gather reads its row numbers there, and the traces agree: in the changed kernel, from 18 us on, 88 gathers begin within an operation of VectorE of 2.2 us with both inputs in SBUF, and each takes 1.89 or more; the other 77 take 1.00 each at most. The same section infers that such an instruction doesn't hold up descriptor generation. Whether the reading of the row numbers or the making of the descriptors was held up here, no run shows; the gather as a whole was.

**The end, -1: wrong by 3.7.** I looked at the paces of PE and VectorE and not at the waits of the last chunk. With PE faster in chunk 14, which has no sums (a last period of 20.1 in e11), VectorE's reduction became the latest thing. PE and VectorE in the changed kernel:

```profile
406.82 1.04 PE L548 MATMUL sums<-feat_b,wt1b_sb 80*128 80x480 f32 x2 [2.19 <-DVE feat_a L420]
...
405.89 0.67 DVE L420 TENSOR_REDUCE feat_a<-cur 128x32 f32<-128x512 f32 x1
```

hid1_of(0) needs reduce1(14), which stands on VectorE behind a low part that PE wants only afterwards. 2.19 us of waiting, then a clock of 0.50, 1.6 us more by the last periods of 23.47 and 21.88. The step that failed is the price itself: 0.7 and 0.2 are differences of pace, and the wait of hid1_of(0) for reduce1(14) stands in it at nothing, without a reason. e11 and e9 take both away (3.4); what is left, 1.3, is about the forecast term.

**Rivals.** Rival 2's overlap came true (the rows of the pair, and e6). Of rival 3 ("the front gives back half: the clock is low, or chunk 1 or 3 comes late") all three parts did; its price, 5 to 7, was right for the front and the stall (5.7). That the time lies near its 440 to 441 is luck in part: the chunks brought 2.3 more than forecast and the end lost 3.7 more. Rival 1's 441 to 443.5 even holds the measured time, and its mechanism (no overlap) is refuted by e6. Rival 4's "about 452" doesn't follow from its own numbers: 26 lost on top of 434.5 would be 460. It is not seen in the changed kernel: split(4) has no wait at 101.02. But e4 and e12 show its mechanism, a chunk's gathers taking longer than PE's chunk, for one chunk: ScalarE waits 9.50 and 5.94 for chunk 4's.

## What to carry to other kernels

When a front is shortened, ask for every resource of the next chunks when it starts and what is queued ahead of it, and take the latest; gains and stalls ahead of such a point are one term and can't be added. A small transfer that is issued in time can still land with the large ones beside it, so the order in which a queue issues large transfers is a lever of its own. In the last chunk, and wherever work is taken from the bounding engine, go through every wait, since an order written for slack turns into the bound there. And before a stretch of a trace is put down to an edit, look at the same stretch in a run that leaves it alone: 1.6 us at the end and 3.6 at chunk 0 came and went here without one.

## What the runs showed of the hardware that I had not expected

- Two float32 matmuls on rows 0 to 63 and 64 to 127, issued one after the other with two passes each, run as A1 B1, A2 B2, each two 0.01 us apart; the pair with its island 1.14 to 1.22 us against 1.72 for two full ones.
- An indirect gather lies on GpSimd for 1.00 us alone, for 1.90 and up when it is issued beside one VectorE operation of 2.2 us with both inputs in SBUF, and for 4.69 and 9.09 beside two and four in a row. It took 1.00 when VectorE stood still (52.95) or read one input from PSUM (e4's 81.41), and went on beside a reduction (the one at 45.76 ended at 47.66, with VectorE reducing from 46.70).
- Beside 3 MB of broadcasts at some 200 GB/s the gathers' queue moved 60 packets in 10 us, then 310 in the next 10.
- The clock was 0.50 (1.2 GHz) from 408 to 410, behind a PE wait of 2.19 us, and 0.58 on the mean from 48.4 to 55.4, behind waits of 2.32 and 2.13. Behind the same wait of 2.19 it stayed at 1.00 in e1 and e8. Behind e2's wait of 1.38 it fell too (0.56), behind e11's two that make 0.9 it stayed at 1.00.
